# Cross-attention and experts on one core: row maxima by a reset running maximum on VectorE in place of mask products on TensorE

## What is computed

```python
x = x + xattn(layernorm(x), ctx)        # 16 heads of 16, causal
x = x + ffn(layernorm(x))               # 8 experts with LoRA, top 2

qp = q @ Wq.T;  k, v = split(latent_kv @ Wkv_expand.T)
scores = einsum('bhqd,bhkd->bhqk', qh, kh) / sqrt(16)
scores = where(tril, scores, finfo.min)
attn = softmax(scores, -1)
out = einsum('bhqk,bhkd->bhqd', attn, vh) @ Wout.T
```

## Time and profile before

| | |
|---|---|
| median of 3 runs | 170.72 us (170.48 to 171.06) |
| profiled execution, its own time | 170.58 us |
| its span | 168.8 us |
| busy: TensorE, weight load | 153.3 us, 118.9 us |
| busy: VectorE, ScalarE, POOL | 105.4 us, 80.1 us, 53.5 us |
| granted TensorE clock, mean | 0.998 |

### The profile page before, as it was taken

One profiled execution on the slowest core, in us unless ns is written; L12 is line 12 of the kernel. 1 busy time (PEld: TensorE's weight loads), 2 busy tenths in 40 slices (PEclk: granted clock), 3 DMA queues, 4 the chain that ended last, 5 costly groups with the idle time before them and its releaser, 6 DMA issues.

```text
span 168.8 us, 3777 instructions
## 1 busy us (share of the span) xinstructions
PE 153.3 (91%) x1481; PEld 118.9 (70%) x1481; DVE 105.4 (62%) x224; ACT 80.1 (47%) x161; POOL 53.5 (32%) x93
## 2 busy tenths in 40 slices
PE   0597999999999999999999997999969989999972
PEld 0365676677777677778778876887758868888961
DVE  2778986859657657835498456555943466444463
ACT  1373557356657776586754617422653022222420
POOL 4276002256378657776740243330000000000000
PEclk9999999999999999999999999999999999999999
DMA  5999940000000000000000185000000594000003
GB/s 148 292 255 229 282 126 2 6 6 0 8 0 8 0 6 2 4 2 4 0 0 4 37 257 209 0 4 0 2 0 4 144 344 137 0 0 0 4 0 124
DMA packets 13042, 11.18 MB, mean 66 GB/s; under 512 B 6457, under 2 KB 10449, under 8 KB 13025
## 3 DMA queue, kind: packets, MB, share of 16 engines
q1 hardware_dynamic: 9584, 7.14, 15.7%
q0 software_dynamic: 544, 2.10, 4.6%
q10 hardware_dynamic: 2896, 1.70, 3.9%
HBM read 9.79 MB, written 1.08 MB: 64 GB/s over the span
## 4 chain that ended last, share of the span: by engine, by line
PE 65%; DVE 14%; DMA 8%; ACT 5%; issue 5%; POOL 1%; DVEq 0%; ACTq 0%
PE bank L798 29%; PE bank L1087 9%; PE bank L908 8%; DMA probsT<-weights 4%; PE bank L894 4%; PE bank L1024 4%; PE bank L915 3%; DVE m_sb L593 2%; DVE h_f L671 2%; DMA x_sb<-in_x 2%; DMA weights<-wT 2%; DVE xhat L552 2%; PE bank L973 2%; ACT silu L410 1%; DVE stats L539 1%
## 5 line engine op out<-in xcount | busy, mean ns | idle before, releaser
L798 PE MATMUL bank<-xT_hi,up_hi 128*128 128x512 f32 x64 | 27.1, 424 | 3.0 <-ACT silu L410 3.0
L318 ACT ACTIVATE h_hi<-h_f 128x512 fp32r<-128x512 f32 x16 | 10.1, 632 | 37.2 <-PE bank L1087 25.9
L295 POOL TENSOR_SCALAR_AFFINE_SELECT probsT<-probsT 128x512 f32<-128x512 f32 x32 | 19.7, 635 | 22.5 <-ACT probsT L391 22.5
L593 DVE TENSOR_REDUCE m_sb<-bank 128x4 f32<-128x512 f32 x32 | 20.4, 685 | 9.4 <-PE bank L908 9.4
L391 ACT ACTIVATE probsT<-bank 128x512 f32<-128x512 f32 x32 | 17.9, 590 | 17.3 <-PE bank L915 17.3
L798 PE MATMUL bank<-xT_hi,up_lo 128*128 128x512 f32 x64 | 25.3, 395 | 0.0
L798 PE MATMUL bank<-xT_lo,up_hi 128*128 128x512 f32 x64 | 25.3, 395 | 0.0
L676 DVE TENSOR_TENSOR h_lo<-h_f,h_hi 128x512 fp32r<-128x512 f32 x16 | 11.4, 713 | 21.0 <-ACT h_hi L318 21.0
L1087 PE MATMUL bank<-dn_hi,h_hi 128*128 128x256 f32 x64 | 18.4, 288 | 1.1 <-DVE h_lo L676 1.0
L915 PE MATMUL bank<-q_f,k_f 32*128 32x128 f32 x256 | 18.6, 283 | 0.0
L798 PEld LDWEIGHTS bank<-xT_hi,up_hi 128*128 128x128 f32 x64 | 12.0, 188 | 8.6 <-ACT silu L410 6.9
(11 more groups left out here) (137 smaller groups left out, 284.4 us busy)
## 6 DMA issues: line engine op xcount, KB each, us to landing
probsT<-weights SPq DMA_DIRECT2D x16, 256.0 KB, 5.5
x_sb<-in_x SPq DMA_DIRECT2D x4, 256.0 KB, 4.8
up_w<-in_L_ffn_gate_up_proj ACTq DMA_DIRECT2D x1, 1024.0 KB, 10.4
up_w<-in_L_ffn_gate_up_proj POOLq DMA_DIRECT2D x1, 1024.0 KB, 7.2
dn_w<-in_L_ffn_down_proj POOLq DMA_DIRECT2D x1, 1024.0 KB, 9.3
out<-x_sb SPq DMA_DIRECT2D x4, 256.0 KB, 2.2
ctx_sb<-in_ctx ACTq DMA_DIRECT2D x2, 128.0 KB, 5.6
wq_raw<-in_L_xattn_Wq ACTq DMA_DIRECT2D x1, 256.0 KB, 5.8
```

Source lines behind the costliest of these rows:

```text
L295: pool.affine_select(out=ch, in_=ch, compare_op=ALU.is_ge, fill=0.0, base=0, pattern=[[0, 4], [1, P]], channel_multiplier=-1).then_inc(S_( ...
L318: act.activation(out_, in_, ACT.Copy, scale=scale).then_inc(S_(done), 1)
L593: dve.reduce_max(m_sb[:, b % 2, :].rearrange("p (u j t) -> p j u t", u=2, t=2)[:, c], S_BANK(b, c)[:, :].rearrange("p (u t n) -> p u t n", ...
L798: last = pe.matmul(out_, a, m, start=start and i == 0, stop=stop and i == len(pairs) - 1, **kw)
```

## The change

- The mask product is gone (and ident_b, causal). Each of a score bank's products writes its own columns.
- `max_chunk` is a scan: from the last column of the bank to the first, state = max(state + resets, score). `resets` (128x512, bf16, made by POOL) is -2^127 on each head's diagonal and 0 elsewhere, so that at the diagonal what came from later keys, and from the head before, is dropped. At key 0 of each head the state is the maximum over the keys up to the diagonal. All 512 states of a bank are written.
- m_sb holds these states, for one item (four banks) and no longer for two; the first scan of item b waits until `max_T(b - 1)` has read them. `max_T` reads every 128th column. `mT_copy` turns the sign.
- The heads' order in the 16 maxima is another one, so the chunks of q_f and k_f, the transfers of `load_max`, `values` and `softmax_divide` use other indices (shown for ScalarE's copies; VectorE's likewise); the division's one multiply becomes two of half the size.

```diff
-        ident_b = sb("ident_b", [P, P], BF16)
...
-        causal = sb("causal", [P, 4, P], BF16)
+        resets = sb("resets", [P, 4 * P], BF16)
...
-        m_sb = sb("m_sb", [P, 2, NH])
+        m_sb = sb("m_sb", [P, NC, 4, P])
...
-        r_den = sb("r_den", [P, 2, NH // 2])
+        r_den = sb("r_den", [P, 2, 2, NH // 4])
...
-                    sp.dma_start(q_f[HD * (1 - u):P:32, 2 * u:2 * u + 2, tokens(b)], mT[u * NH // 2:(u + 1) * NH // 2, :])\
+                    sp.dma_start(q_f[HD * (1 - u):P:32, u:NC:2, tokens(b)], mT[u:NH:2, :])\
...
-            link(pool.affine_select(out=ident[:, :], in_=ident[:, :], compare_op=ALU.not_equal, fill=1.0,
-                                    base=0, pattern=[[-1, P]], channel_multiplier=1))
-            pool.tensor_copy(ident_b[:, :], ident[:, :]).then_inc(S_("ident_made"), 1)
+            pool.affine_select(out=ident[:, :], in_=ident[:, :], compare_op=ALU.not_equal, fill=1.0,
+                               base=0, pattern=[[-1, P]], channel_multiplier=1).then_inc(S_("ident_made"), 1)
...
-            link(pool.memset(causal[:, :, :], 0.0))
-            pool.affine_select(out=causal[:, :, :], in_=causal[:, :, :], compare_op=ALU.is_ge, fill=MASKED,
-                               base=0, pattern=[[0, 4], [-1, P]], channel_multiplier=1).then_inc(S_("causal_made"), 1)
+            link(pool.memset(resets[:, :], 0.0))
+            diagonals = resets[:, :].rearrange("p (h n) -> p h n", h=4)
+            pool.affine_select(out=diagonals, in_=diagonals, compare_op=ALU.not_equal, fill=MASKED, base=0,
+                               pattern=[[0, 4], [-1, P]], channel_multiplier=1).then_inc(S_("resets_made"), 1)
...
                 for u in range(2):
-                    spread(k_f[:, 2 * u, pair(p)], K_BANK(p, 0)[:, 0:PN], u, first[:, 1 - u:2 - u], "k_by_act")
+                    spread(k_f[:, u, pair(p)], K_BANK(p, 0)[:, 0:PN], u, first[:, 1 - u:2 - u], "k_by_act")
...
                 for u in range(2):
-                    spread(q_f[:, 2 * u, pair(p)], Q_BANK(p, 0)[:, 0:PN], u, zero_col[:, :], "q_by_act")
+                    spread(q_f[:, u, pair(p)], Q_BANK(p, 0)[:, 0:PN], u, zero_col[:, :], "q_by_act")
...
-                copy(mT[:, :], M_BANK(b), "mT_copied")
+                copy(mT[:, :], M_BANK(b), "mT_copied", -1.0)
...
                 dve.wait_ge(S_("s_ready"), NC * b + c + 1)
-                if b >= 2 and c == 0:
-                    dve.wait_ge(S_("mT_ready"), b - 1)
-                dve.reduce_max(m_sb[:, b % 2, :].rearrange("p (u j t) -> p j u t", u=2, t=2)[:, c],
-                               S_BANK(b, c)[:, :].rearrange("p (u t n) -> p u t n", u=2, t=2), AX.X, negate=True)\
-                    .then_inc(S_("max_done"), 1)
+                if b == 0 and c == 0:
+                    dve.wait_ge(S_("resets_made"), 1)
+                if b and c == 0:
+                    dve.wait_ge(S_("mT_ready"), b)
+                dve.tensor_tensor_scan(m_sb[:, c, :, :].rearrange("p h n -> p (h n)")[:, ::-1], resets[:, ::-1],
+                                       S_BANK(b, c)[:, ::-1], MASKED, ALU.add, ALU.max).then_inc(S_("max_done"), 1)
...
-            on = bank[5][:, :].rearrange("p (u h w) -> p u h w", u=2, w=32)
-            o_heads = o_nat[:, :, :].rearrange("p (h u) d -> p u h d", u=2)
+            on = bank[5][:, :].rearrange("p (t u j w) -> p t u j w", t=2, u=2, w=32)
+            o_heads = o_nat[:, :, :].rearrange("p (t j u) d -> p t u j d", t=2, u=2)
...
                     dve.wait_ge(S_("o_T"), b)
-                dve.reciprocal(r_den[:, :, :], on[:, :, :, HD]).then_inc(S_("r_den_ready"), 1)
+                dve.reciprocal(r_den[:, :, :, :], on[:, :, :, :, HD]).then_inc(S_("r_den_ready"), 1)
                 dve.wait_ge(S_("r_den_ready"), b + 1)
-                dve.tensor_tensor(o_heads, on[:, :, :, 0:HD], r_den[:, :, :, None].to_broadcast([P, 2, NH // 2, HD]), ALU.mult)\
-                    .then_inc(S_("o_nat_ready"), 1)
+                for t in range(2):
+                    last = dve.tensor_tensor(o_heads[:, t], on[:, t, :, :, 0:HD],
+                                             r_den[:, t, :, :, None].to_broadcast([P, 2, NH // 4, HD]), ALU.mult)
+                last.then_inc(S_("o_nat_ready"), 1)
...
                             pe.wait_ge(S_("max_done"), n - 3 if s == 1 else n - 1)
-                        pe.matmul(S_BANK(s, j)[:, :], ident_b[:, :], causal[:, :, :].rearrange("p h n -> p (h n)"),
-                                  start=True, stop=True, skip_group_check=True)
                 if t is not None:
...
-                                             start=False, stop=True, skip_group_check=True)
+                                             start=True, stop=True)
...
-                pe.transpose(M_BANK(b), m_sb[:, b % 2, :], ident[:, :]).then_inc(S_("mT_ready"), 1)
+                pe.transpose(M_BANK(b), m_sb[:, :, :, 0].rearrange("p j c -> p (j c)"), ident[:, :]).then_inc(S_("mT_ready"), 1)
...
-                        h = 8 * (c % 2) + 2 * j + c // 2
+                        h = 8 * (c // 2) + 2 * j + c % 2
...
-            pe.wait_ge(S_("causal_made"), 1)
```

More of the change, by code:

```diff
@@ L568, in k_copy @@
                 for u in range(2):
-                    spread(k_f[:, 2 * u + 1, pair(p)], K_BANK(p, 1)[:, 0:PN], u, first[:, 1 - u:2 - u], "k_by_dve")
+                    spread(k_f[:, 2 + u, pair(p)], K_BANK(p, 1)[:, 0:PN], u, first[:, 1 - u:2 - u], "k_by_dve")
             def q_copy(p):
@@ L573, in q_copy @@
                 for u in range(2):
-                    spread(q_f[:, 2 * u + 1, pair(p)], Q_BANK(p, 1)[:, 0:PN], u, zero_col[:, :], "q_by_dve")
+                    spread(q_f[:, 2 + u, pair(p)], Q_BANK(p, 1)[:, 0:PN], u, zero_col[:, :], "q_by_dve")
             def merge(n):
```

## The result

| | before | with the change |
|---|---|---|
| median, us | 170.64 (170.48 to 171.06, 4 runs) | 178.43 (178.11 to 179.6, 4 runs) |
| profiled execution, its span | 170.58, 168.8 | 178.37, 176.5 |
| granted TensorE clock, mean | 0.998 | 0.979 |

The ratio is 1.0465, with a 95% interval from 1.0414 to 1.0516: slower by 7.8 us. The prediction was 178.6 us, with a range from 174.8 to 181.4.

The account below looks back on a forecast made before the run. TensorE's lines headed the chain; longer scans would lengthen its loop with VectorE. 170.58 us + 2.7 before pair 1 + 5.0 in the halves + 0.3 behind the last pair = 178.6 us; range 174.8 to 181.4.

Parts of the forecast that it names:

- Duration of the scan: One VectorE scan of a 512-column bank: two steps a column, 1.20 us, where a reduction takes 0.68.
- rival A: Scans take one step a column, as short as reductions: 164.6 us, faster than before; chance 0.11.
- Start: Everything up to pair 1: masks gone but scans longer, pair 1 at 28.68 us instead of 25.99, +2.7.
- pair 1: First of twelve counted pairs of VectorE row-maximum instructions on two score banks; 25.99 us before, forecast at 28.68.
- Halves: The eleven stretches between starts of the twelve pairs, each half a batch item: 46.95 us instead of 41.9, +5.0.
- the round (a): Scans, pickup and score group in turn, one of three candidates for a half's length: 3.76 us, 4.01 with max_T between.
- pickup: From the end of a scan pair to TensorE's first score product: 0.25 us, 0.06 for signal, 0.19 for weights.
- Behind pair 12: The stretch after the last counted pair's start: max_T of item 7 waits for two merges, +0.3 us.
- The small edits: Split division: 0.1 us more, eight times, counted in half 4; scale -1 copies, head order, load_max strides, resets: nothing.
- Rival B: VectorE is full but waits nowhere: its extra work against 13.7 us free gives +3.7, 174.3 us; chance 0.05.
- C: Every scan lies on the path and the masks come back: +9.8, new wait 1.5, up to 181.9 us; chance 0.08.
- What I said of the waits: TensorE's waits at L908 for VectorE's m_sb would be longest in total, some 10 us.

## Why the prediction was right, point by point

- **Duration of the scan**, 1.20 us predicted, 1.203 measured. The rate of two steps a column held in every form that was tried, and with every second column scanned the kernel took rival A's way. That the two steps come from two operations that depend on each other is the prediction's argument; no run varied the operations.
- **Start**, +2.7: pair 1 at 28.78 instead of the predicted 28.68, +2.8.
- **Halves**, 46.95 predicted, 46.26 measured. Halves 2 and 4, VectorE's own work, came at 5.10 and 5.36 for 5.12 and 5.41. In the round (a) the pickup was mis-sized: a score product starts 0.10 us behind the second scan (57.65 against 57.55), not 0.25. The row of the weight load below shows it: it waits for the scan too and starts at 57.62, and the product follows 0.03 us behind, so the load's 0.19 us don't stand ahead of it. The group takes 1.16 us. So halves 5, 7, 9 and 11 have 3.6 for 3.76, 0.16 to 0.18 too much four times; half 3, with the low clock, has 3.69. At two of the seven waits, 27.28 and 44.30, the pickup was 0.35 us; why is not known. Against that, max_T costs 0.31 to 0.34 and not 0.25, and half 6 came at 4.67 for 4.48. Part of my accuracy is luck: these errors have opposite signs.

```profile
57.62 0.22 PEld L908 LDWEIGHTS bank<-k_f,q_f 32*128 32x128 f32 x2 [1.38 <-DVE m_sb L594]
```

- **Behind pair 12**, +0.3: max_T of item 7 was issued 3.61 us after the pair for 3.35 before, +0.26 as predicted; the whole stretch is 0.56 us longer. VectorE waited 2.75 us there for the routing weights' transfer where it had waited 2.34; that transfer was not examined.
- **Sum**: 2.8 + 4.3 + 0.6 = 7.7 us on the span, 8.0 predicted.
- **The small edits**, 0.1 us in half 4 and nothing elsewhere: the two multiplies of the division take 0.49 us for 0.42. No run undid one of them alone: as the kernel is written, the transposition reads the 16 maxima with one stride, and the new order of heads and the two multiplies follow from it. The run with every second column scanned bounds all of them together, with the new wait: 166.75 beside 166.94 us for the kernel without masks, which has none of them; by the intervals they cost less than some 1.5 us together.
- **Rival A** was the right way for a fast scan but sized wrong, at 164.6 us for 166.75: its step "pair 1 comes 1.6 us earlier" did not look at what else TensorE waits for there, the transfer of the maxima. With that wait gone the kernel with reductions takes 165.7 us, still 1.1 above; the late first reduction of some executions may be a part of that.
- **Rival B** (no waits, 174.3) and **C** (everything on the path, 181.9) failed on the halves: VectorE is 89% busy and not full, and halves 1, 6 and 10 are 0.1 to 0.45 us shorter than before, 9 and 11 only 0.3 longer. I had foreseen over 90%.
- **What I said of the waits** was half right: TensorE's for the scan is 7.2 us in all where I said 10, and it is TensorE's longest but not the longest of all: ScalarE's, POOL's and VectorE's own for ScalarE (h_lo for h_hi, 20.7 us) are longer, and the longest, ScalarE's for the down products, is what it was (25.7 us, 25.9 before).

## What to carry to other kernels

Ask what an instruction carries from one column to the next before you take the rate of its neighbours for it: this scan, with an addition and a maximum, took 1.20 us for 512 columns where a reduction or an addition takes 0.68, and so cost more than the masks did. When two engines hand two buffers back and forth, sum one round of it and each engine's own work for each half and take the longest; idle time of an engine in such a loop is no room for more work. And before a gain at the start is counted, look at the next transfer that has to land.

## What the runs showed that I had not expected

The granted clock fell, twice in each profiled execution of the changed kernel. Three windows (columns as in the earlier trace rows, clock behind POOL):

```profile
24.00:26.00 2.00, 2.00 (x10) 1.18 (x10) 2.00 (x3) 0.37 (x2) 0.00 (x0) 0.53 0.06 12
36.00:38.00 2.00, 2.00 (x41) 1.34 (x38) 1.93 (x7) 1.22 (x3) 0.00 (x0) 0.53 0.03 8
38.00:40.00 2.00, 2.00 (x24) 1.31 (x16) 2.00 (x3) 0.82 (x3) 1.82 (x4) 0.62 0.02 4
```

TensorE was at some 0.5 to 0.6 of its 2.4 GHz there, so mostly at 1.2 GHz. Before the first fall it had idled 2.36 us for the scans of item 0 (18.4 to 20.7 us). Before the second it had waited 0.57 and 1.05 us for VectorE between 32.4 and 35.3 us; its products with v took 1.91 us there, where the kernel before takes 1.07. In the kernel before no slice fell. In the first run with two buffers it came later:

```profile
42.00:44.00 2.00, 2.00 (x18) 1.21 (x14) 1.84 (x2) 1.60 (x3) 1.06 (x2) 0.50 0.00 0
```

and half 3 lasted 4.34 us, with VectorE idle 1.97 us before its pair, against 3.64 in the other execution of the same kernel. This 0.7 us is as large as the saving that was to be measured. It may be part of why the times of two buffers spread from 176.5 to 178.7 us while the rows tell the kernels apart; only two of those executions have rows.

The second was a transfer of 4 KB that took 4.55 us beside the weights' loads. In the kernel before it landed at about the same time, but TensorE was busy with mask products in front of it, and only its weight load waited, for 0.4 us.
